# Experts' phase of an attention and mixture-of-experts kernel: written out, six heads' products on VectorE, blocks' rows added two blocks at a time

## The reference, cut to what matters

```python
score = jnp.einsum('bsid,bsjd->bsij', Q, K) / jnp.sqrt(jnp.float32(D_K))   # 16 x 16 per token
attn = jax.nn.softmax(score, axis=-1)
out = jnp.einsum('bsij,bsjd->bsid', attn, V)                               # first branch
...
x = x + _mla(_rmsnorm(x, g1), Wq, Wdkv, Wuk, Wuv, Wo)                      # second branch
hid = jax.nn.silu(jnp.einsum('td,edh->teh', t, w1))                        # experts, 256 -> 512
ye = jnp.einsum('teh,ehd->ted', hid, w2)                                   # 512 -> 256
out = jnp.einsum('te,ted->td', combine, ye)                                # two experts a token
```

## Time and profile before

| | |
|---|---|
| median of three runs | 3068.91 us |
| the profiled execution | 3062.26 us, of which the span from first to last instruction is 3060.5 us |
| mean granted clock of PE in it | 0.933 of full speed |
| busy share of the span | PE 84%, DVE 76%, POOL 76%, ACT 51% |
| phase 4: first DMA to last scatter issued | 2245.1 to 3022.6 us |
| phase 5: first store issued to the end of the span | 3031.9 to 3060.5 us |
| phase 4, 2300 to 2955 us: PE waits for rows | 154.8 us in 29 waits |
| the same stretch: ACT waits for a block's qkv | 150.3 us in 29 waits |
| the same stretch: DVE waits for POOL's products | 71.1 us in 25 waits |
| DVE row sums and reciprocal of a block | 0.41 and 0.25 us |

### The profile page before, as it was taken

The page is one execution under the profiler, slowest core; times in us unless marked ns, Lnnn a source line. Parts: engine busy times, 40 slices in busy tenths (PEclk is TensorE's granted clock), DMA queues, the critical chain, the costliest instruction groups (busy, mean ns, idle before and its releaser), DMA issues. The chain is left out here.

```text
span 3060.5 us, 59749 instructions
## 1 busy us (share of the span) xinstructions
PE 2571.4 (84%) x21356; PEld 1316.2 (43%) x21356; DVE 2334.0 (76%) x3621; ACT 1572.3 (51%) x2325; POOL 2328.0 (76%) x1230
## 2 busy tenths in 40 slices
PE   7998978999999999999999999766757768777782
PEld 4544432333333333333333333255646656666662
DVE  4567858999999999998999984045639888988860
ACT  2322236777777767777677777622323333333330
POOL 5443359788988889888988889746748888888882
PEclk9999999999999999999999999877778989889886
DMA  5886541323332223332233311387566667666766
GB/s 195 273 269 203 180 149 52 85 51 86 82 88 77 64 84 82 90 79 64 82 83 85 75 40 42 97 259 252 171 186 171 164 167 167 170 163 164 173 160 165
DMA packets 296054, 404.89 MB, mean 132 GB/s; under 512 B 32040, under 2 KB 221832, under 8 KB 295560
## 3 DMA queue, kind: packets, MB, share of 16 engines
q1 hardware_dynamic: 264360, 357.80, 39.1%
q0 software_dynamic: 31200, 39.73, 7.6%
q10 hardware_dynamic: 256, 4.19, 0.4%
HBM read 251.16 MB, written 158.23 MB: 134 GB/s over the span
## 5 line engine op out<-in xcount | busy, mean ns | idle before, releaser
L1044 DVE TENSOR_REDUCE p_piece_max<-p_ring 128x1 f32<-128x512 f32 (+3 forms) x2160 | 1293.7, 654 | 137.4 <-PE p_ring L157 67.7
L1102 ACT ACTIVATE p_probs<-p_st 128x1024 f32<-128x1024 f32 (+3 forms) x1280 | 1079.0, 897 | 413.8 <-PE p_st L1165 216.6
L1165 PE MATMUL p_st<-unit_q,unit_k 64*128 64x512 bf16 (+3 forms) x3520 | 434.6, 349 | 42.1 <-ACT p_probs L1102 25.4
L1183 PE MATMUL p_pv<-p_probs,unit_vg 128*32 128x512 f32 (+3 forms) x3520 | 412.0, 542 | 0.0
L1806 POOL TENSOR_TENSOR p_pv<-p_pr,p_qkv 128x1024 f32<-128x1024 f32 (+1 forms) x96 | 403.1, 4206 | 1.4 <-ACT p_pr L1936 1.4
L982 POOL TENSOR_TENSOR p_terms<-p_head_p,p_head_in 128x4096 f32<-128x4096 f32 x32 | 348.5, 10890 | 0.1
L1822 POOL DMA_INDIRECT acc<-p_y,p_rows x142 | 224.8, 1583 | 105.2 <-issue 42.0
L2003 PE MATMUL p_y_ps<-p_w,p_hid 128*128 128x256 f32 x1136 | 300.4, 425 | 3.4 <-ACT p_hid L1949 3.3
L170 PE MATMUL p_ring<-unit_k,unit_q 64*128 64x512 bf16 (+3 forms) x1600 | 271.7, 353 | 27.9 <-DVE p_piece_max L1044 25.4
L961 POOL TENSOR_TENSOR p_terms<-p_head_in 128x4096 f32<-128x4096 f32 x32 | 283.4, 8856 | 8.2 <-POOL p_head_s L969 4.4
L1990 PE MATMUL p_hid_ps<-p_rT,p_w 128*128 128x256 f32 x1136 | 259.8, 382 | 7.1 <-issue 4.3
(11 more groups left out here) (184 smaller groups left out, 3610.0 us busy)
## 6 DMA issues: line engine op xcount, KB each, us to landing
p_w<-ffn_w SPq DMA_DIRECT2D x142, 512.0 KB, 5.6
qk_parts<-p_parts SPq DMA_DIRECT2D x64, 384.0 KB, 3.4
head_qkv<-p_heads SPq DMA_DIRECT2D x16, 1536.0 KB, 6.5
p_rows<-rows_by_expert SPq DMA_DIRECT2D x71, 258.0 KB, 3.7
unit_q<-qk_parts SPq DMA_DIRECT2D x132, 128.0 KB, 3.2
unit_k<-qk_parts SPq DMA_DIRECT2D x132, 128.0 KB, 3.6
v_padded<-p_vx SPq DMA_DIRECT2D x16, 1024.0 KB, 8.2
p_head_in<-head_qkv SPq DMA_DIRECT2D x32, 384.0 KB, 4.0
```

The lines of the kernel that those rows point to most:

```text
L1044: nc.vector.tensor_reduce(piece_max[:, n % 2, h:h + heads, i, pc], ring_ps[g % RING][:, 0:heads * width].rearrange("p (h k) -> p h k", h=h ...
L1102: nc.scalar.activation(probs[:, 2 * turn_of(s, i) + u, :, 0:width], st_ps[u][:, :, 0:width], ACT.Exp).then_inc(probs_done, 1)
L1165: last = nc.tensor.matmul(st_ps[u][:, half, 0:width], k6[s][rows, PAIR * second + u, kt * P:(kt + 1) * P], q6[s][rows, PAIR * second + u, ...
L1183: last = nc.tensor.matmul(pv_ps[hh * VW:(hh + 1) * VW, skip:CT], vg[s][:, kt, hh * VW:(hh + 1) * VW], probs[:, 2 * turn_of(s, i) + hh % PA ...
```

## The change

Only phase 4 changes; all of the arithmetic stays.
- The loops are written out for all 71 tiles and 32 blocks on all engines, with fixed numbers in place of registers, and `wait_apart` becomes a plain wait.
- `pr` holds ten heads (HP = 10). ACT's exp is two instructions, ten heads to SBUF and six to PSUM, in place of the scores. POOL's `weigh` multiplies heads 0 to 4 behind one `add_tile` and 5 to 9 behind the next. DVE multiplies the last six from PSUM (`weigh_tail`) and takes the row sums in two parts.
- The sums over POOL's and DVE's products go to a new PSUM bank `o_ps`, and the division reads them there.
- `add_block` goes. SP stores a block's 128 rows plainly to `attn_rows` in DRAM behind the loads of tile 2m + 7 (`store_block`). Every fourth tile, from tile 10 on, POOL adds two stored blocks to `acc` with one DMA from DRAM to DRAM, 256 KB in pieces of 8 KB (`add_pair`), when both stores and all earlier scatters have landed; two of the five heads of that tile are multiplied behind it, and the next `add_tile` waits for its landing.
- `qkv` has QB = 3 buffers. Block m is loaded behind the loads of tile 2m - 1 (before: 2m + 1), and waits for the products of block m - 3. ACT copies q of block m at tile 2m, as before, but at the start no longer waits for the first two blocks before its first SiLU.

```diff
-    RB = 4
+    RB, QB = 4, 3
+    HP = 10
+    SPAN = 64
+    STARTS = [m * SPAN // NB for m in range(NB + 4)]
+    PIECES = {2: (5, 5), 3: (4, 3, 3)}
+    WEIGHED = {n: (m, heads, heads.stop == HP) for m in range(NB) for n, heads in pieces(m)}
+    ADDED = {STARTS[2 * k + 4] + 2: k for k in range(NB // 2)}
+    STORED = {STARTS[m + 2] + 3: m for m in range(NB)}
+    LOADED = {max(0, STARTS[m] - 1): m for m in range(QB, NB)}
+    COPIED = {STARTS[m]: m for m in range(NB)}
+    SHIFTED = {STARTS[m + 1]: m for m in range(NB)}
...
-        qkv = sb("p4_qkv", [P, 2, 3, D])
+        qkv = sb("p4_qkv", [P, QB, 3, D])
-        pr = sb("p4_pr", [P, 2, H, H])
+        pr = sb("p4_pr", [P, 2, HP, H])
+        o_ps = bank("p4_o_ps")
...
+            def load_block(m):
+                if m >= QB:
+                    sp.wait_ge(pv_done, m - QB + 1)
+                    sp.wait_ge(tail_done, m - QB + 1)
+                sp.dma_start(qkv[:, m % QB, :, :].rearrange("p i d -> p (i d)"), head_qkv[block_of(m, 1)]
+                             ).then_inc(qkv_loaded[m % QB], 16)
+
+            def store_block(m):
+                sp.wait_ge(oh_done, m + 1)
+                sp.dma_start(attn_rows[block_of(m, 1)], oh[:, m % 2, :, :].rearrange("p i d -> p (i d)")
+                             ).then_inc(oh_stored[m % 2], 16)
...
+            for n in range(N_TILE):
...
+                if n in LOADED:
+                    load_block(LOADED[n])
+                if n in STORED:
+                    store_block(STORED[n])
...
-            def add_block(m, u, n, tiles):
-                wait_apart(pool, oh_done, m + 1, apart)
-                wait_apart(pool, y_added, 16 * RT * tiles, apart)
-                nc.gpsimd.dma_start(acc[bass.ds(n * P, P), :], oh[:, u, :, :].rearrange("p i d -> p (i d)"),
-                                    accum_op=ALU.add).then_inc(oh_added, 16)
+            def add_pair(k, tiles):
+                for u in range(2):
+                    pool.wait_ge(oh_stored[u], 16 * (k + 1))
+                pool.wait_ge(y_added, 16 * RT * tiles)
+                n = block_of(2 * k, 1)
+                rows_of_pair = lambda a: a.rearrange("(r s) d -> r (s d)", s=8)
+                nc.gpsimd.dma_start(rows_of_pair(acc[n * P:(n + 2) * P, :]),
+                                    rows_of_pair(attn_rows[n:n + 2, :, :].rearrange("a p d -> (a p) d")),
+                                    accum_op=ALU.add, max_dma_last_dim=4 * 8 * D).then_inc(pair_added, 16)
+                pairs[0] += 1
+
+            for n in range(N_TILE):
+                if n:
+                    add_tile(n - 1)
+                weighed = WEIGHED.get(n)
+                if n not in ADDED:
+                    if weighed:
+                        weigh(*weighed)
+                    continue
+                if weighed:
+                    m, heads, last = weighed
+                    weigh(m, slice(heads.start, heads.stop - 2), False)
+                add_pair(ADDED[n], n)
+                if weighed:
+                    weigh(m, slice(heads.stop - 2, heads.stop), last)
...
+            def weigh_tail(m):
+                u, count = m % 2, H - HP
+                dve.wait_ge(exp_done, m + 1)
+                nc.vector.tensor_reduce(psum[:, 0:HP], pr[:, u, :, :], AX_X, ALU.add)
+                nc.vector.tensor_reduce(psum[:, HP:], s_ps[u][:, HP:, :], AX_X, ALU.add).then_inc(psum_done, 1)
+                nc.vector.tensor_tensor(
+                    pv[:, u, HP:, :, :],
+                    s_ps[u][:, HP:, :].unsqueeze(2).to_broadcast([P, count, DH, H]),
+                    qkv[:, m % QB, 2, :].rearrange("p (j d) -> p d j", d=DH).unsqueeze(1).to_broadcast([P, count, DH, H]),
+                    ALU.mult).then_inc(tail_done, 1)
...
-                nc.vector.tensor_reduce(oh[:, u, :, :], pv[:, u, :, :, :], AX_X, ALU.add).then_inc(pv_added, 1)
...
+                nc.vector.tensor_reduce(o_ps[:, u * D:(u + 1) * D].rearrange("p (i d) -> p i d", d=DH), pv[:, u, :, :, :],
+                                        AX_X, ALU.add).then_inc(o_done, 1)
...
+                nc.scalar.activation(pr[:, u, :, :], sm[:, 0:HP, :], ACT.Exp)
+                nc.scalar.activation(s_ps[u][:, HP:, :], sm[:, HP:, :], ACT.Exp).then_inc(exp_done, 1)
```

More of the change, by code:

```diff
@@ L1812, in weigh_values, with add_tile @@
                     ins.then_inc(pv_done, 1)
-            def add_tile(n, i, blocks):
-                wait_apart(pool, y_copied, n + 1, apart)
-                if not (static(n) and n == 0):
-                    wait_apart(pool, y_added, 16 * RT * n, apart)
-                if not (static(blocks) and blocks == 0):
-                    wait_apart(pool, oh_added, 16 * blocks, apart)
+            pairs = [0]
+            def add_tile(n):
+                pool.wait_ge(y_copied, n + 1)
+                if n:
+                    pool.wait_ge(y_added, 16 * RT * n)
+                if pairs[0]:
+                    pool.wait_ge(pair_added, 16 * pairs[0])
@@ L1915, in _ @@
+            for m in range(NB + 2):
+                if m >= 2:
+                    finish(m - 2)
+                if 0 < m <= NB:
+                    weigh_tail(m - 1)
+                if m < NB:
+                    score(m)
         @block.scalar
         def _(act):
-            act.sem_inc(silu_done, 2)
             def copy_rows(n):
                 act.wait_ge(rT_done, n + 1)
-                act.wait_ge(hid_done, 2 * n)
+                if n:
+                    act.wait_ge(hid_done, 2 * n)
@@ new lines, in _ @@
+            copy_rows(0)
+            for n in range(N_TILE):
+                for k in range(2):
+                    act.wait_ge(hid_done, 2 * n + k + 1)
+                    if n:
+                        act.wait_ge(y_done, n)
+                    nc.scalar.activation(hid[:, 2 * k:2 * k + 2, :].rearrange("p k t -> p (k t)"), hid_ps[k][:, :],
+                                         ACT.Silu).then_inc(silu_done, 1)
+                if n + 1 < N_TILE:
+                    copy_rows(n + 1)
+                if n in SHIFTED:
+                    probabilities(SHIFTED[n])
+                if n in COPIED:
+                    copy_q(COPIED[n])
+                act.wait_ge(y_done, n + 1)
+                if n >= RB:
+                    act.wait_ge(y_added, 16 * RT * (n - RB + 1))
+                for t in range(RT):
+                    last_copy = nc.scalar.activation(y[:, n % RB, t, :], y_ps[t][:, 0:D], ACT.Copy,
+                                                     scale=rows[:, n % RB, t, D:D + 1])
+                last_copy.then_inc(y_copied, 1)
```

260 lines of the change are left out of this document (90 added, 170 removed).

## The result

The changed kernel took 2976.19 us (median of 4 runs, 2963.62 to 2980.33) against 3071.62 us before on the same chip: ratio 0.9675, 95% interval 0.9649 to 0.9701, so 95 us less by the medians and 100 by the ratio. The prediction was 3024 us, 45 us less than before. The sign held, and so did the wide range (2965 to 3074); the forecast band of 3000 to 3052 was missed, and the gain was twice what was forecast. The profiled execution took 2972.77 us.

The account below looks back on a forecast made before the run. Serial landings of additions into acc, lengthened by weights, were taken to bound the kernel. Groups -38 us, tiles ahead -8, start -3 and tail +4 gave -45: 3024 us in the median; forecast 3000 to 3052, range 2965 to 3074.

Parts of the forecast that it names:

- What bounds the kernel: Experts' phase: no engine full; serial landings of additions into acc set the pace, 2 to 3 us a step from weights.
- The start of the weights: SP's queue in the experts' phase: weights go out just as each scatter does, every time; steps of 9.1 us.
- Heads to DVE: Value products: POOL's floor of a tile falls to 7.2 us; DVE's block takes 17.0 us and costs nothing.
- Division in PSUM: DVE's division by the row sums, one input now in PSUM: 0.42 us, where it took 4.86.
- case D: Rival: DVE's division stays at 4.9 us and DVE sets 10.7 us a tile: 3044 us, chance 0.06.
- Pair addition: DRAM-to-DRAM addition of two blocks every four tiles, on the serial chain: 7.0 us, ends 4.0 and 12.4.
- the free step: Scatter behind each pair, with no weights beside it: 6.4 us by landing, 7.2 by POOL; 7.2 taken.
- Case A: Rival: the pair's landing beside the weights is the new wait, 12.4 us a step: 3110 us, chance 0.12.
- SP's queue freed: SP's qkv load: with three buffers it is hardly held by POOL's product, a wait of 257 us before.
- Written out, start, tail: Written-out loops: nothing, ends -10 and +15 us; start of the experts' phase -3 us; its tail +4 us.
- Case C: Rival: pairs of 4.0 us and steps of 8.4, qkv and stores unseen: 2942 us, chance 0.22.

Follow-up runs that it names:

- the third weights' buffer: Changed kernel with three buffers of weights in place of two, each load waiting for PE on tile n-3, not n-2: 3018.76 us, ratio 0.9818.
- the one with single additions: Changed kernel, but each block is added to acc by itself from SBUF, without stores or pairs: 3059.91 us, ratio 0.994.
- the hold: SP sends weights only after POOL's first head behind each scatter; on the changed kernel with blocks added singly: 2965.57 us, ratio 0.9632.
- the held kernel: Changed kernel with SP holding the weights until POOL's first head behind each scatter is done: 2940.81 us, ratio 0.9556.
- the fastest one: Changed kernel with two pairs added every eighth tile, v laid out plainly by ACT, and weights held behind POOL's first head: 2904.13 us, ratio 0.9435.
- the kernel that is only written out: Changed kernel with heads, pairs, PSUM sums and qkv order undone, leaving written-out loops and plain waits: 3076.7 us, ratio 0.9996.

## Why the prediction was right or wrong

**What bounds the kernel: right.** Serial landings with the weights' share on top, and POOL's own work level with them.

**The start of the weights: wrong, and this is the step that failed.** "So the weights will go out just as each scatter does, every time" gave steps of 9.1 us. They began less than 2 us behind in only 3 of 51, and the 13 groups measured give 9.23, 7.47 and 8.48 us, 8.4 on average, for the three steps of a group that I had at 9.1. That is 2.1 us a group, some 30 us in 14. SP's wait for PE holds the weights until about 3.4 us or more behind the scatter in most of the second and third of these steps, and the prediction puts nothing for that wait. The assumption's own error was shown by making it true: the third weights' buffer, which takes that wait away, gave steps of 9.3, 8.8 and 9.2 us and 56 us less than before, where the forecast was 45. The prediction held the rows that pointed to it, against the earlier trace rows (6.31 us with weights 3.9 us late), and took the early start without walking SP's queue through one group of the changed kernel.

**The steps keep themselves.** Where a scatter lands late, its landing releases SP's rows, PE has long been done, and the weights go out behind the next scatter, which then lands late too. Where POOL sets the step, PE is later within it, and the weights with it. SP's waits for PE fit this: 124.8 us in the changed kernel, 29.9 us in the one with single additions (2300 to 2880 us). This reading would explain why heads and pairs together bring twice the sum of each, but it is argued and not shown. What the hold shows is that the weights' place is enough (95 us by it alone, with single additions).

**Heads to DVE: right in kind, DVE's cost low.** POOL's floor is 7.2 us as worked out. DVE's block is 4.42 + 4.43 + 4.36 + 2.77 + 3 x 0.42 + 0.31 + 0.25 + 0.25 = 18.1 us, not 17.0, for the steps of 16 elements. It cost nothing at 19.2 us for two tiles; it is the bound where the weights are left out, and nearly so in the held kernel (488.7 of 500 us), so this error would have mattered in a prediction of either.

**Division in PSUM: duration right, worth nothing.** 0.42 us, as taken. But case D's price was wrong too: undone alone, the division takes 1.43 us, not 4.9. That the shorter products of POOL are the reason is likely and not shown.

**Pair addition: too dear.** 7.0 us was put down, 6.05 measured in the 13 groups; with the free step at 7.2 as worked out, that is 1.0 us a group, 14 in all. Case A did not come. The last pair, with no weights in flight:

```profile
2927.82 0.86 POOL L1840 DMA_DIRECT2D acc<-attn_rows  x1 [2.67 <-DMA acc<-p_y,p_rows]
2932.58 1.62 POOL L1830 DMA_INDIRECT acc<-p_y,p_rows  x1 [3.91 <-DMA acc<-attn_rows]
```

It is 4.76 us a step; one block singly is 4.0. The estimate from the Trainium skill (DMA: Bandwidth & Descriptors, "Anatomy of one DMA"), 2.6 us, is too low even with no load beside it: POOL spends 0.86 us on the descriptors and then waits 3.91 us for the landing.

**SP's queue freed: wrong.** The wait for POOL's product is 148 us in 27 waits, where I had it gone. The product of block m - 3 that I called finished before the next landing ends 7 us behind the scatter, as POOL's step of 7.2 us itself ends. It matters little: the load in its old place costs 10 us or nothing, and the weights behind this wait still go out 2.9 us behind the scatter, in the steps of 9.2 us. The weights that are late enough are those that wait for PE.

**Written out, start, tail.** Nothing, as taken, for the first; the idle microsecond at a loop's edge shows in no row either. Up to the first scatter the start brought none of its 3 us: from phase 3's last scatter to the first of phase 4 it is 27.7 us before and 28.1 after. Groups make up 81 of the 94.5 us; ahead of them and behind them lie the other 13, where I had 8 ahead, 4 lost behind and the 3 of the start.

**The cases.** Case C gave 2991 for short steps alone; with a pair a microsecond cheaper, 14 us, that is the time measured. Its number was near and its mechanism was not: the steps aren't 8.4 us each with qkv and stores unseen, but a mixture of 7.2 and 9.4, and qkv's step is the long one. That is luck. (Its full sum, -109, -16, -3 and +4, gives 2945 and not 2942.)

**What stays open.** What goes on between the first issue and 3.4 us that is so sensitive, the descriptors being written, the reads or the additions, no run tells apart. POOL's two issues end some 3.4 us behind the first one's start (2599.58 to 2603.01 above), which points to the descriptors and proves nothing. Nor is it settled whether the weights slow the scatter or only stand ahead of its second half in the DMA engines' order. A hold that is earlier than one head's product was not tried, nor a load sent on purpose just ahead of the scatter.

## What to carry over

Where small accumulating DMAs stand in a serial chain, as here, the place of a large load against them can be worth more than its earliness: look in the timelines how far behind each such DMA the load begins, sort the steps by it, and then hold the load on purpose with a semaphore that the same engine gives. Before costing an edit that frees a queue, walk the queue through one whole step of the changed kernel, for every wait in it: one that seems to cost nothing, like SP's for PE here, may be what keeps two transfers apart. If two edits together bring far more than each alone, or edits that take work away bring nothing, look for a transfer that moved.

## What was not expected of the hardware

- 1 MB of weights begun within 2.6 us behind a 256 KB accumulating scatter lengthens its step by about 2 us (8.9 to 9.1 against 7.2). The cost fades up to 3.4 us. None shows beside POOL's 7.2 us when the load begins 0.3 to 1.5 us ahead of the scatter (7.27, six steps), and none 4.5 us behind it (7.41 and 6.31 us with single additions, against 7.49 and 6.25 with no weights). Held so, the kernel with single additions went from ratio 0.994 to 0.9632.
- An SBUF operand read in steps of 16 elements costs DVE 2.77 against 1.75 us for 1536 elements, and POOL 4.05 against 3.45 us for 1280, in products whose result is written in a row.
- A 256 KB addition from DRAM to DRAM in pieces of 8 KB is a step of 4.8 us alone and 5.4 to 7.5 beside weights, hardly more than a block half its size from SBUF (4.0, and 6.18 beside weights).
- The granted clock of PE was 0.88 in the window of before, 0.91 in the changed kernel, 0.95 in the fastest one. PE's busy share doesn't account for it: the kernel that is only written out has 0.88 at 77% busy and, with the hold, 0.95 at 78% (2350 to 2850 us).
